# First attention: scores added as differences of key tiles onto the scores of two steps before

## What is computed

```python
# x (4, 1024, 256), layer-normalised; 8 heads of 64; keys and values from a latent of 64
q = (x @ Wq.T).reshape(b, t, 8, 64)
kv_latent = x @ Wkv_down.T
k = (kv_latent @ Wk_up.T).reshape(b, t, 8, 64)
v = (kv_latent @ Wv_up.T).reshape(b, t, 8, 64)
attn = softmax(einsum('bqhd,bkhd->bhqk', q, k) / 8)
out = einsum('bhqk,bkhd->bqhd', attn, v).reshape(b, t, 512)
x = x + out @ Wo.T
...        # then a feed-forward layer, a second attention, a second feed-forward layer
```

## Time and profile before

| what | value |
|---|---|
| runs, median (lowest to highest) | 2409.69 us (2409.66 to 2413.33), 3 runs |
| span of the profiled execution | 2414.0 us |
| the first attention in it | scores from 43.8 to 776.4 us, next stage from 798.8 us |
| PE busy over the span | 2336.0 us (97%) |
| VectorE busy | 1515.8 us (63%) |
| ScalarE busy | 1345.0 us (56%) |
| POOL busy | 1045.1 us (43%) |

### The profile page before, as it was taken

One profiled execution on the slowest core, in us unless ns is written; L12 is line 12 of the kernel. 1 busy time (PEld: TensorE's weight loads), 2 busy tenths in 40 slices (PEclk: granted clock), 3 DMA queues, 4 the chain that ended last, 5 costly groups with the idle time before them and its releaser, 6 DMA issues.

```text
span 2414.0 us, 39029 instructions
## 1 busy us (share of the span) xinstructions
PE 2336.0 (97%) x15265; PEld 1450.1 (60%) x15265; DVE 1515.8 (63%) x1934; ACT 1345.0 (56%) x1787; POOL 1045.1 (43%) x674
## 2 busy tenths in 40 slices
PE   6989999999999899999999999999999999999999
PEld 4545555555555788888888887444444444443588
DVE  6877787787784324312222223779989989989364
ACT  3555555554454444444444443478778778777743
POOL 1656776776677346556556456030000000000354
PEclk8999999999999999999999999899999999999999
DMA  1211321312112455565555556433433333332232
GB/s 43 80 69 54 97 71 63 97 59 66 63 54 64 145 166 183 172 198 180 179 187 193 169 190 199 123 94 75 89 83 71 85 77 74 85 83 55 61 118 82
DMA packets 156836, 259.04 MB, mean 107 GB/s; under 512 B 37004, under 2 KB 97292, under 8 KB 156300
## 3 DMA queue, kind: packets, MB, share of 16 engines
q1 hardware_dynamic: 156652, 256.53, 35.7%
HBM read 206.52 MB, written 60.68 MB: 111 GB/s over the span
## 4 chain that ended last, share of the span: by engine, by line
PE 61%; ACT 2%; DMA 1%; DVE 1%; issue 1%; SPq 0%; POOL 0%; POOLq 0%; ACTq 0%
PE m_R L129 45%; PE m_O L129 11%; PE m_X L129 4%; DMA m_K<-bounce_k 1%; ACT m_P L1702 1%; PE m_X L226 1%; DVE m_mraw L1851 1%; ACT m_OS L1709 0%; PE m_X L2065 0%; SPq L1560 0%; DVE m_ln_x L205 0%; PE m_R L226 0%; DMA bounce_k<-m_comp 0%; ACT m_comp L1722 0%; DVE m_ln_stat L183 0%
## 5 line engine op out<-in xcount | busy, mean ns | idle before, releaser
L1851 DVE TENSOR_REDUCE m_mraw<-m_R 128x2 f32<-128x1024 f32 x512 | 622.5, 1221 | 73.0 <-PE m_R L129 61.1
L1702 ACT ACTIVATE m_P<-m_R 128x1024 f32<-128x1024 f32 x512 | 523.6, 1025 | 154.8 <-PE m_R L129 154.5
L589 ACT ACTIVATE a_P<-a_S 128x1024 f32<-128x1024 f32 x256 | 248.9, 1024 | 217.8 <-PE a_S L129 217.8
L129 PE MATMUL m_O<-m_P,m_V 128*17 128x256 f32 x4096 | 331.4, 396 | 4.5 <-ACT m_P L1702 2.6
L887 POOL TENSOR_TENSOR a_accp<-a_accp,a_P 128x1024 f32<-128x1024 f32 x96 | 249.8, 2602 | 15.2 <-ACT a_P L589 6.0
L1956 POOL TENSOR_TENSOR m_act0l<-m_xf,m_act0h 128x512 fp32r<-128x512 f32 x128 | 164.8, 1290 | 210.8 <-ACT m_xf L1764 112.9
L129 PE MATMUL a_O<-a_P,a_V 128*64 128x512 f32 x1024 | 248.0, 605 | 4.4 <-ACT a_ON L597 4.4
L129 PE MATMUL m_R<-m_act0h,wt 128*128 128x512 f32 x640 | 251.3, 393 | 0.0
L129 PE MATMUL m_R<-m_act0l,wt 128*128 128x512 f32 x640 | 250.4, 391 | 0.0
L720 DVE TENSOR_REDUCE a_mraw<-a_X 128x2 f32<-128x1024 f32 x164 | 199.9, 1219 | 78.5 <-PE a_X L129 78.3
L129 PE MATMUL m_R<-m_Q,m_K 64*128 64x512 f32 x800 | 201.5, 500 | 2.8 <-DVE m_mraw L1851 2.5
(11 more groups left out here) (250 smaller groups left out, 4251.7 us busy)
## 6 DMA issues: line engine op xcount, KB each, us to landing
wt<-wcopy SPq DMA_DIRECT2D x176, 512.0 KB, 3.4
m_K<-bounce_k SPq DMA_DIRECT2D x96, 128.0 KB, 5.5
m_ln_x<-x SPq DMA_DIRECT2D x23, 512.0 KB, 4.2
a_tile<-in_L_ffn_tiles SPq DMA_DIRECT2D x22, 512.0 KB, 4.6
wcopy<-in_L_ffn_tiles SPq DMA_DIRECT2D x22, 512.0 KB, 5.3
x<-xres SPq DMA_DIRECT2D x78, 128.0 KB, 2.8
m_Q<-bounce_q SPq DMA_DIRECT2D x150, 64.0 KB, 2.3
xres<-x SPq DMA_DIRECT2D x64, 128.0 KB, 2.7
```

What stands on the lines that cost most here:

```text
L129: return pe.eng.matmul(out, lhsT, rhs, start=start, stop=stop, skip_group_check=True)
L589: act.eng.activation(P[n % NP][:, :, :], psS[n % 2][:, :, :], ACT.Exp, scale=SCALE).then_inc(s_exp)
L1702: act.eng.activation(P[h % 4][:, :, :], pair(key)[:, :, :], ACT.Exp, scale=SCALE).then_inc(R.free(key))
L1851: dve.eng.tensor_reduce(mraw[u % 2][:, at, :], pair(key)[:, :, :], AX.X, ALU.max).then_inc(R.free(key))
```

## The change

From step t = 2 of a unit on, the two passes that a step shares with the step two before it are not made anew. `psS[n % 2]` still holds the scores of step `n - 2`, maxima subtracted; ScalarE has read them, and PE adds onto them (the first pass no longer overwrites) the product of the queries with the difference of the two key tiles. The difference has a high part `Dh` = rounded (`Kh` of tile t less `Kh` of tile t - 2), stored in `shared.wt`, and a low part, which replaces tiles 2 to 7 of `Kl` in place. So steps 2 to 7 of a unit have three passes instead of four; steps 0 and 1 stay as they are.

POOL makes the differences (`differ`), 11 instructions for each sequence. Those of sequence 0 stand before POOL's loop, those of the next sequence in the five turns from (8b + 6, 3) to (8b + 7, 3), after that turn's adds. PE waits for them (`s_differ`) ahead of step 2 of each sequence, and SyncE's loads into `shared.wt` wait for the scores that read it.

```diff
--- before.py
+++ after.py
@@ -284,6 +284,10 @@
 
     def values_at(u, j):
         return u // UB + 1 if u // UB + 1 < B and (u % UB, j) == (6, 2) else None
+
+    def differ_at(u, j):
+        b, i = u // UB + 1, 4 * (u % UB) + j - 27
+        return (b, i) if b < B and 0 <= i < 5 else None
 
     def query_at(u, j):
         return u + 2 if j == 0 and u + 2 < NU else None
@@ -363,6 +367,8 @@
         Qh, Ql = [[p.sb(f"Q{j}{i}", [128, 512], F32R) for i in range(3)] for j in "hl"]
         M = [p.sb(f"M{i}", [128, 512], F32R) for i in range(3)]
         spread = p.sb("spread", [128, 128], F32R)
+        rest = p.sb("rest", [128, 384])
+        Dh = [shared.wt[i][:, 0:T - 256] for i in (0, 1, 0, 2)]
         V = [p.sb(f"V{i}", [128, NT, 64]) for i in range(2)]
         P = [p.sb(f"P{i}", [128, NH, 512]) for i in range(NP)]
         wkd = [p.sb(f"wkd{i}", [128, 2, 128], F32R) for i in range(2)]
@@ -390,6 +396,7 @@
         s_ident, s_identr, s_fill = p.sem("ident"), p.sem("identr"), p.sem("fill")
         s_raw = [p.sem(f"raw{i}") for i in range(4)]
         s_prod, s_whi, s_wlo = p.sem("prod"), p.sem("whi"), p.sem("wlo")
+        s_differ = p.sem("differ")
         s_lathi, s_qhi, s_max = p.sem("lathi"), p.sem("qhi"), p.sem("max")
         s_rows = [p.sem(f"rows{i}") for i in range(3)]
         s_scores, s_exp, s_pv, s_os = p.sem("scores"), p.sem("exp"), p.sem("pv"), p.sem("os")
@@ -534,6 +541,7 @@
                     move_inverse(u - 1)
             for i in range(3):
                 sp.wait_ge(s_copy, 16 * LOWS0)
+                sp.wait_ge(s_scores, (3 * UB * NT, 2 * UB * NT, STEPS)[i])
                 sp.eng.dma_start(f32(shared.wt[i][:, :]), wcopy[i]).then_inc(s_wt, 16)
             store(*out_at(NU - 1, 3))
             for b, t in TAIL:
@@ -895,6 +903,40 @@
                 pool.wait_ge(s_oh, out_index(b, t) + 1)
                 pool.eng.tensor_tensor(osp[t % 2][1][:, :, :], ON[b % 2][:, :, cols], f32(osp[t % 2][0][:, :, :]), ALU.subtract).then_inc(s_ol)
 
+            def differ(b, i):
+                kh, kl, dh = f32(Kh[b % 2][:, :]), Kl[b % 2], Dh[b]
+                klf = f32(kl[:, :])
+
+                def op(to, x, y, how=ALU.subtract):
+                    pool.eng.tensor_tensor(to, x, y, how).then_inc(s_differ)
+
+                def before(count):
+                    pool.wait_ge(s_differ, 11 * b + count)
+                if i == 0:
+                    for half in range(2):
+                        pool.wait_ge(*X.emptied(("latent", b, half)))
+                    if b >= 2:
+                        pool.wait_ge(s_scores, NT * UB * (b - 1))
+                    op(dh, kh[:, 256:T], kh[:, 0:T - 256])
+                    return
+                first, count = (640, 1) if i < 3 else (256, 6)
+                here, back = slice(first, first + 384), slice(first - 256, first + 128)
+                if i in (1, 3):
+                    before(count)
+                    op(rest[:, :], kh[:, here], f32(dh)[:, back])
+                    before(count + 1)
+                    op(rest[:, :], rest[:, :], kh[:, back])
+                else:
+                    before(count + 2)
+                    op(rest[:, :], rest[:, :], klf[:, here], ALU.add)
+                    before(count + 3)
+                    pool.wait_ge(*X.filled(("values", b)))
+                    op(kl[:, first + 256:first + 384], rest[:, 256:384], klf[:, first:first + 128])
+                    before(count + 4)
+                    op(kl[:, first:first + 256], rest[:, 0:256], klf[:, first - 256:first])
+
+            for i in range(5):
+                differ(0, i)
             for m, (u, j) in enumerate(turns()):
                 if out_at(u, j):
                     out_low(*out_at(u, j))
@@ -903,6 +945,8 @@
                 if m:
                     for n in (2 * m - 2, 2 * m - 1):
                         add(n)
+                if differ_at(u, j):
+                    differ(*differ_at(u, j))
                 if norm_at(u, j) and norm_at(u, j)[1] == 4:
                     norm.power(pool, norm_at(u, j)[0])
             scale_out(NU - 2)
@@ -973,11 +1017,16 @@
                     pe.wait_ge(*X.emptied(("latent", b, half)))
                 pe.wait_ge(s_rows[u % 3], 32 * (u // 3 + 1))
                 pe.wait_ge(s_exp, n - 1)
-                terms = ((Kh[b % 2], cols, Qh[u % 3]), (Kh[b % 2], cols, Ql[u % 3]), (Kl[b % 2], cols, Qh[u % 3]), (spread, slice(0, 128), M[u % 3]))
+                if t < 2:
+                    terms = ((Kh[b % 2], cols, Qh[u % 3]), (Kh[b % 2], cols, Ql[u % 3]), (Kl[b % 2], cols, Qh[u % 3]), (spread, slice(0, 128), M[u % 3]))
+                else:
+                    pe.wait_ge(s_differ, 11 * b + 11)
+                    since = slice(128 * t - 256, 128 * t - 128)
+                    terms = ((Dh[b], since, Qh[u % 3]), (Dh[b], since, Ql[u % 3]), (Kl[b % 2], cols, Qh[u % 3]))
                 for i, (w, c, x) in enumerate(terms):
                     for h in range(NH):
                         rows = slice(64 * h, 64 * h + 64)
-                        ins = mm(pe, psS[n % 2][:, h, :], w[rows, c], x[rows, :], i == 0, i == 3)
+                        ins = mm(pe, psS[n % 2][:, h, :], w[rows, c], x[rows, :], t < 2 and i == 0, i == len(terms) - 1)
                 ins.then_inc(s_scores)
 
             def weigh(n):
```

## The result

The changed kernel takes 2416.3 us (median of 16 runs, 2409.69 to 2420.79) against 2410.42 us for the kernel before (16 runs): a ratio of 1.0023, 95% interval [1.0016, 1.0030], so it is 5.9 us slower. The forecast was a difference of -0.6 us, within 0.2% of no change. The time lies inside the range given (2398 to 2419 us), near the rival called "Slower: POOL's lateness at the borders" (2418.0 us).

A forecast was written before the change was run, and what follows sets the result against it. PE was taken as the bound, with VectorE's chain of reductions close beneath. A gain of 7.6 us and a price of 7.0 us gave -0.6 us on the median 2409.69: 2409.1 us, range 2398 to 2419 us.

The forecast's parts named there:

- Slower: POOL's lateness at the borders: All three sequence borders cost 3.8 us of lateness plus 1.5 us of clock loss, less 7.6: 2418.0 us, chance 0.16.
- A turn gains 0.09 to 0.15 us, and not 0.46.: Where PE's second pass of maxima waits for VectorE's first reduction, dropping two passes of scores saves only this much a turn.
- gain of 7.6: Total saving in us forecast from dropping 192 passes of scores, 44.2 us at face value; bounds 5 and 10.
- Rival 2: PE is the bound, as its busy share says; all 192 passes count in full: 2365.5 us, chance 0.04.
- rival 4: The clock swings in every unit since PE runs empty 0.2 us a turn; 31 dips of 1.5 us: 2455.6 us, chance 0.02.
- A sequence costs 10.5 us: POOL's time for one sequence's key differences; for sequence 0 hidden in POOL's idle 38.2 us before its first add.
- wait 3.1 us: At unit 7's end PE's sums wait this long for POOL's late last add; 3.5 us for each of the first two borders.
- turns without maxima: Of the last six turns, five lose two passes; three gain 0.46 us each, 1.4 us together (2.3 if all five count).
- the term for POOL: Price of the differences added to POOL, mostly lateness at sequence borders: 7.0 us, bounds 1 and 11.
- VectorE's own delay I put at 0.4 us, once a sequence.: VectorE's adds meet POOL more often; the delay to VectorE counts in a j = 3 turn, 0.4 us.
- Before unit 24 POOL has 5.94 us to spare and the turns are longer: I take 0 there.: At the third border POOL's lateness was forecast to cost 0, with 3.5 us as the upper bound.
- rival 3: POOL's lateness costs 3.8 us at each of three borders and each wait drops the clock, 1.5 us: 2418.0 us, chance 0.16.

## Why the prediction was wrong

Right were these steps:

- *"A turn gains 0.09 to 0.15 us, and not 0.46."* `B` stands at +1.91 or +1.98 as said, j = 3 turns at 4.21 to 4.28 us, j = 2 turns with `project_out` at 6.23, as before; PE's busy share fell to 95.9 in 100, not below 95. The gain of 7.6 measured 6.7 alone. In its parts it was less exact: with the three passes alone the j = 1 turns gained 3.9 us (1.9 said), the j = 3 turns 3.3 (3.0 said), and the j = 0 turns, which lose no pass, grew by 1.2, so part of the agreement is luck. Rival 2 and rival 4 fell with the same runs: 36.5 us come only when the reductions are cut, and the short idling dropped no clock.
- *"A sequence costs 10.5 us", sequence 0 hidden, `s_differ` about 0.* The first sequence's differences ran from 25.1 to 36.1 us, ahead of the first add at 49.3.
- *PE's sums "wait 3.1 us", at each of the first two borders.* With POOL's work alone the sums waited 2.60 and 2.58 us, and their turns grew by 6.05 us together where 6.2 was said. In the changed kernel they waited 3.02 and 0.88. The 3.02 is a match by luck: L899 ended 2.1 us later than I said (243.56, not 241.5), and PE came to the sums 2.2 us later too (240.59 instead of 238.4). The 0.88 is small because VectorE's add had already delayed PE in (15,3); where that add didn't wait, in the kernel with the one-input reduction, it was 2.86.

Not exact, without weight in the sum, were the *turns without maxima*. Five got 0.45 us shorter, and from the last scores to the next stage it took 24.3 us instead of 22.4. 1.0 of these 1.9 us come ahead of the last sums, which POOL's last add holds up; the rest lies behind them, where the clock stood at 1.2 GHz for longer. The kernel with three passes and no differences takes 24.1 us there as well. 0.4 us are left of the 1.4 I had taken.

Wrong was the term for POOL: 7.0 us said, 13.7 measured alone. Three steps of it failed.

- *"VectorE's own delay I put at 0.4 us, once a sequence."* In the changed kernel it was 0.9, 1.9 and 1.95 us: 2.14, 3.10 and 3.17 instead of 1.22; with POOL's work alone 0.9 each time. I had read that POOL's add takes 3.35 us beside VectorE's, 1.0 more, and split the loss to POOL's side. What decides is which of the two is in work when the other comes, and POOL's lateness moved its longest instructions, two adds of 2.4 us back to back, across VectorE's add, where POOL used to be idle. The trace of before had the price already. The groups by line from 0 to 850 us give VectorE's add of j = 0, which does meet POOL, a mean of 1859 ns:

```profile
L746 DVE TENSOR_TENSOR a_accd<-a_accd,a_P 128x1024 f32<-128x1024 f32 x32 | 59.5, 1859 | 5.3 <-ACT a_P L589 5.3
```

Its longest took 3.35 us, against 1.22 alone. Of the 41 times in that trace, between 60 and 760 us, that such an instruction (L746 or L771) began with over 0.3 us left of a POOL instruction, it ended 1.08 or 1.09 us after POOL's end in 40; the one that didn't had met a power instruction of LayerNorm (L200). The rule of the Trainium skill that I had set beside the sum (SBUF — State Buffer, "Who interferes with whom") has the loser waiting for the whole instruction of the other; the two-column add of 2.25 us and the one-input reduction of 1.21 agree with it in both directions. I had applied it to the 384-column differences, for 1 us in all, and not to the adds that they delay.
- *"Before unit 24 POOL has 5.94 us to spare and the turns are longer: I take 0 there."* The spare time is real, but the chain of the third border doesn't go through L899. It goes through VectorE's add into the ring of maxima: 1.95 us in (23,3), and behind the 2.90 us of wait a dip, with 2.76 us. At the second border it is that chain too which costs most: 1.66 in (15,3), 0.79 at the sums. So of the waits' 8.8 us some 4.2 came by VectorE.
- *The clock was left out of the sum*, and stood in rival 3 alone, with 0.16. Turns with passes at 1.2 GHz hold 8.3 us of the profiled execution, and 2.6 us with POOL's work alone. By my own reading of the earlier trace rows, a wait of 1.82 us had gone with a dip; I had forecast two waits of 3.1 us and should have priced a dip behind each. The two longest border waits (3.02 and 2.90) had one, the 1.75 at 419.75 none. The three dips that lie elsewhere (3.8 us) stay open: the kernel with three passes and the one with three groups in the pause have none, the one with four groups there has two, at 162.8 and 739.7.

Rival 3 came close in time (2418.0) by another sum than the one that was paid: it has 3.8 us of POOL's lateness and a dip of 1.5 us at each of three borders. The clock behind the waits was its part that held; the way through VectorE's add is in no rival.

That a better place would repair it was shown: same passes, same differences, 2406.33 us.

## What to carry over

An engine that is 99% busy may be waiting in disguise: before a pass is priced by its length, the first thing behind it that has another releaser has to be found. Work added to an engine with slack is priced by what its lateness then lies beside, not only by who waits for its result; put it into the pause ahead of the busy stretch, and the same work cost 3.2 us instead of 12.6. The size of such a collision may already stand in the trace of before, at another line of the same kind. And where a forecast holds a wait of 2.5 us or more on TensorE, a dip of the clock behind it belongs in the sum.

## What was unexpected in the hardware

- A VectorE add with two SBUF inputs waits for the end of the POOL instruction in work, whatever its own size: 128x2 took 2.25 us. POOL waits in the same way: its add of 128x2 took 1.06 us beside VectorE's.
- A VectorE reduction with one SBUF input, 128x1024, took 1.21 us beside the same POOL instruction, and an add with one input in PSUM kept its 0.42 us. But one SBUF input is not enough by itself: a cast of 128x1024 from int32 to fp32 (L776, five times) took 0.69 us with POOL idle and 1.40 to 2.91 us with POOL at work.
- Regular idling of PE, 0.2 us in each turn, left the clock at 1.00. In the eleven profiles with full reductions, from 60 to 760 us, nine of the eleven waits of 2.5 to 3.1 us had a dip of 3.4 or 6.8 us beginning at them (2.88 and 2.91 us had none), and nine of 52 waits of 1.5 to 2.1 us.
- The same 192 passes are worth 6.7 or 36.5 us, by the length of another engine's reductions.
